# A graph network on one core: indirect transfers ordered by landings in place of clears

## What is computed

```
h = maximum(layernorm(x), 0)
# block 1 (layer 0 below): an equivariant message for each edge, summed at its destination
R = relu(edge_weight[:, None] @ w1 + b1) @ w2 + b2      # 384 radial weights for each edge
Y = spherical_harmonics(edge_attr_3)
msg = tensor product of R, Y and h[src]                 # 32 values
x = x + zeros.at[dst].add(msg)
# block 2 (layers 1 to 3 below): three graph convolutions, 32 -> 128 -> 128 -> 32
h = maximum(layernorm(x), 0)
h = relu(segment_sum((h @ W)[src] * norm[:, None], dst) + b)   # three times
x = x + h
```

## Time and profile before

| | |
|---|---|
| median of 3 runs | 5780.96 us (5775.5 to 5783.35) |
| span of the profiled execution | 5779.7 us |
| its own time beside the span | the trace gives the span alone, first to last instruction; it is 1.3 us below the median |
| busy share of the span | POOL 85%, PE 74%, DVE 62%, PE weight loads 54%, ACT 47% |
| indirect transfers on POOL, L782 | 3616, 1006 ns each |
| clears on POOL, L762 | 3616, 341 ns each |
| DMA queue of the indirect transfers | 109.02 MB in 115712 packets, 10.3% of the 16 engines' time |
| granted TensorE clock, mean over the span | 0.82 of full speed |

### The profile page before, as it was taken

One profiled execution on the slowest core, in us unless ns is written; L12 is line 12 of the kernel. 1 busy time (PEld: TensorE's weight loads), 2 busy tenths in 40 slices (PEclk: granted clock), 3 DMA queues, 4 the chain that ended last, 5 costly groups with the idle time before them and its releaser, 6 DMA issues.

```text
span 5779.7 us, 179150 instructions
## 1 busy us (share of the span) xinstructions
PE 4258.6 (74%) x62463; PEld 3147.7 (54%) x62464; DVE 3608.0 (62%) x8469; ACT 2702.7 (47%) x6550; POOL 4889.1 (85%) x7276
## 2 busy tenths in 40 slices
PE   5777777777777777755555555889898889766666
PEld 3444444444444444444444444778787778554554
DVE  8777777777777777776666666333333334555555
ACT  4444444444444444466666666344444444433333
POOL 7888888888888888768888888688888889588886
PEclk9999999999999999955555555899989999767767
DMA  3111111111111111333332332332333333444444
GB/s 87 33 33 33 33 33 31 33 33 33 33 33 32 32 33 33 36 71 77 77 77 77 77 77 71 114 90 85 91 91 85 91 91 100 119 119 126 122 127 107
DMA packets 494970, 400.88 MB, mean 69 GB/s; under 512 B 269575, under 2 KB 454828, under 8 KB 493537
## 3 DMA queue, kind: packets, MB, share of 16 engines
q10 hardware_dynamic: 146996, 207.67, 10.6%
q0 software_dynamic: 115712, 109.02, 10.3%
q1 hardware_dynamic: 231536, 74.48, 5.9%
HBM read 375.52 MB, written 15.29 MB: 68 GB/s over the span
## 4 chain that ended last, share of the span: by engine, by line
POOL 50%; issue 40%; PE 5%; POOLq 2%; DVE 2%; DMA 1%; ACT 0%; DVEq 0%; SPq 0%
POOL rows L782 29%; POOL pause L762 21%; POOLq L761 2%; PE radial L2067 2%; PE psX L2082 1%; PE psT L2082 1%; PE sums L2153 1%; PE radial L2209 0%; DMA table<-arena 0%; PE radial L2222 0%; DMA rows<-table,idx 0%; DMA xn<-in_x 0%; POOLq L760 0%; PE radial L2008 0%; DVE rows L1827 0%
## 5 line engine op out<-in xcount | busy, mean ns | idle before, releaser
L782 POOL DMA_INDIRECT rows<-table,idx x3616 | 3636.6, 1006 | 803.0 <-POOL pause L762 483.7
L762 POOL MEMSET pause<- 128x256 f32 x3616 | 1234.8, 341 | 2.5
L1942 PEld LDWEIGHTS sums<-scratch,onehot 128*64 128x64 f32 x9408 | 789.7, 144 | 465.0 <-DVE scratch L1377 228.6
L2067 PE MATMUL radial<-arena,shared 128*32 128x96 bf16 (+1 forms) x31200 | 926.4, 266 | 154.2 <-DVE shared L1613 75.1
L1942 PE MATMUL sums<-scratch,onehot 128*64 128x264 f32 (+1 forms) x9408 | 984.1, 356 | 32.6 <-DVE scratch L1377 26.2
L2067 PEld LDWEIGHTS radial<-arena,shared 128*32 128x32 bf16 (+1 forms) x31200 | 664.8, 116 | 294.4 <-issue 72.0
L2153 PE MATMUL sums<-onehot,rows 128*128 128x80 f32 (+1 forms) x2844 | 371.0, 298 | 576.7 <-DMA rows<-table,idx 571.8
L1007 ACT CAST scratch<-radial 128x480 bf16<-128x480 f32 x860 | 476.9, 555 | 665.7 <-PE radial L2067 657.6
L1360 DVE TENSOR_TENSOR scratch<-radial,shared 128x768 f32<-128x768 f32 x784 | 743.4, 948 | 0.0
L1927 PE MATMUL radial<-shared 64*128 64x384 f32 x3136 | 730.5, 546 | 0.0
L880 ACT COPY shared<-rows 128x192 f32<-128x192 f32 x196 | 89.4, 456 | 1264.1 <-DMA rows<-table,idx 1262.9
(11 more groups left out here) (237 smaller groups left out, 5969.3 us busy)
## 6 DMA issues: line engine op xcount, KB each, us to landing
scratch<-places_d ACTq DMA_DIRECT2D x242, 800.0 KB
rows<-table,idx POOLq DMA_INDIRECT x3616
shared<-in_edge_weight SPq DMA_DIRECT2D x390, 128.0 KB, 2.9
idx<-in_src SPq DMA_DIRECT2D x451, 4.0 KB
table<-arena SPq DMA_DIRECT2D x24, 256.0 KB, 2.8
table<-arena SPq DMA_DIRECT2D x2, 1176.0 KB, 10.6
accT<-in_edge_attr SPq DMA_DIRECT2D x2, 1152.0 KB
table<-arena SPq DMA_DIRECT2D x24, 96.0 KB, 2.0
```

Of the source, the lines that this page charges most:

```text
L762: nc.gpsimd.memset(pause[:, :], 0.0).then_inc(made, 1)
L782: (pool.indirect_dma_start(rows_3[:, r, j, :] if n in (1, 3) else rows[:, r, j, 0:WIDTH[n]], None, tables[n], bass.IndirectOffsetOnAxis(ap ...
L1942: last = nc.tensor.matmul(there, onehot[:, u % 2, 4 * h + t, 0:SW], taken_from, start=(h + q + part == 0), stop=(h == 1 and q == 1 and par ...
L2067: last = nc.tensor.matmul(d, from_src[n][:, h, i, t, :], table_of(n, s), start=True, stop=True, tile_position=(0, 32 * i))
```

## The change

The clear, its tile and its counter go. In their place POOL waits ahead of each transfer until the last but one has landed (IN_FLIGHT = 2). To know this of each, the transfers count up two semaphores in turn (LANES = 2): the even tiles j one, the odd ones the other, and no longer one for each place in `rows`. The registers `landed` hold the counts in the loop; in the written-out steps they are constants. Those who wait for a whole group (SP ahead of `load_idx`, ACT, PE) now wait for both semaphores, with `wait_gathered`.

```diff
--- before.py
+++ after.py
@@ -59,7 +59,8 @@
 MSGW = TAIL0 + OUTS
 SUMW = 8 * OUTS
 PAD_REL = -1000.0
-PAUSE = 256
+LANES = 2
+IN_FLIGHT = 2
 assert NG % UNROLL == 0 and PTAIL * KS == ETAIL and PTAIL <= P and NG == 2 * NB
 
 
...
-        pause = sb("pause", [P, PAUSE])
...
@@ -347,7 +347,7 @@
         table_out = sems("table_out", 2)
         chunk_out = sems("chunk_out", 4)
         idx_in = [sem(f"idx_in{u}") for u in range(UNROLL)]
-        gathered = [sem(f"gathered{u}") for u in range(UNROLL)]
+        gathered = sems("gathered", LANES)
         ew_in = sems("ew_in")
         hid_ready = sems("hid_ready", 2)
         rows_copied = sems("rows_copied")
@@ -463,9 +463,11 @@
             n = len(sems)
             return sems[event % n], step.times(step.groups * each // n, before * (UNROLL * each // n) + event // n + 1)
 
-        def rows_gathered(step, n, u, plus):
-
-            return step.times(step.groups // UNROLL * 16 * TPG, 16 * TPG * (rounds_before(n) + u // UNROLL + plus))
+        def wait_gathered(eng, n, step, u):
+
+            each = 16 * TPG // LANES
+            for lane in range(LANES):
+                eng.wait_ge(gathered[lane], step.times(step.groups * each, each * (sum(GATHERED[:n]) + u + 1)))
 
         def bucket_count(n, step, v, plus=0):
 
@@ -614,7 +616,7 @@
                 at = step.times(step.groups * GE, u * GE)
                 if n > 0 or not (first and u < UNROLL):
 
-                    sp.wait_ge(gathered[r], rows_gathered(step, n, u, 0))
+                    wait_gathered(sp, n, step, u - UNROLL)
                 if n == 0 and (step.it * UNROLL + u == NG - 1 if step.peeled else False):
                     d = idx[0:PTAIL, r, 0:KS]
                     s = src[(NG - 1) * GE:E].rearrange("(p k) -> p k", k=KS)
@@ -748,18 +750,18 @@
 
 
             turn = [pool.alloc_register(f"turn_pool{u}") for u in range(UNROLL)]
-            pauses = pool.alloc_register("pauses")
-
-            def pause_between(step, n, u, j):
-
+            landed = [pool.alloc_register(f"landed{lane}") for lane in range(LANES)]
+
+            def wait_landed(step, n, u, j):
+
+                lane = (j - IN_FLIGHT) % LANES
                 if step.peeled:
-                    before = TPG * (sum(GATHERED[:n]) + step.it * step.groups + u) + j
-                    if before:
-                        pool.wait_ge(made, 9 + before)
+                    before = TPG * (sum(GATHERED[:n]) + step.it * step.groups + u) + j - IN_FLIGHT
+                    if before >= 0:
+                        pool.wait_ge(gathered[lane], 16 * (before // LANES + 1))
                 else:
-                    pool.wait_ge(made, pool.snap(pauses))
-                    pool.reg_add(pauses, pauses, 1)
-                nc.gpsimd.memset(pause[:, :], 0.0).then_inc(made, 1)
+                    pool.wait_ge(gathered[lane], pool.snap(landed[lane]))
+                    pool.reg_add(landed[lane], landed[lane], 16)
 
             def gathers(n):
                 def body(step, first, last):
@@ -779,10 +781,10 @@
                             pool.reg_add(turn[r], turn[r], 1)
                         for j in range(TPG):
                             col = j % 2 * KS + j // 2
+                            wait_landed(step, n, u, j)
                             (pool.indirect_dma_start(rows_3[:, r, j, :] if n in (1, 3) else rows[:, r, j, 0:WIDTH[n]], None, tables[n],
                                                      bass.IndirectOffsetOnAxis(ap=idx[:, r, col:col + 1], axis=0))
-                                 .then_inc(gathered[r], 16))
-                            pause_between(step, n, u, j)
+                                 .then_inc(gathered[j % LANES], 16))
                     if n == 0 and first:
                         pool.wait_ge(centred, 2)
                         nc.gpsimd.memset(xn[:, NB - 1, :], 0.0).then_inc(pads, 1)
@@ -804,7 +806,9 @@
                         pool.wait_ge(chunk_out[c % 4], chunks_stored(n, c))
                 for u in range(UNROLL):
                     pool.reg_mov(turn[u], 2 * (LOOP[n][0] // UNROLL - 1) if n else 0)
-                pool.reg_mov(pauses, 9 + TPG * (sum(GATHERED[:n]) + LOOP[n][0]))
+                for lane in range(LANES):
+                    pool.reg_mov(landed[lane], 16 * ((TPG * (sum(GATHERED[:n]) + LOOP[n][0]) + lane) // LANES
+                                                     - (1 if lane >= LANES - IN_FLIGHT else 0) + 1))
                 sweep(pool, body, n)
 
             for n in range(NLAYER):
@@ -873,7 +877,7 @@
                     nc.scalar.activation(hid[:, u % 2, :, :], ew_row[:, u % 2, :].rearrange("c (p k) -> c k p", k=KS),
                                          ACT.Relu, bias=b1c[:, :], scale=w1c[:, :]).then_inc(hid_ready[u % 2], 1)
 
-                    act.wait_ge(gathered[u], rows_gathered(step, 0, u, 1))
+                    wait_gathered(act, 0, step, u)
                     if not (first and u < 2):
                         act.wait_ge(*when(prods_done, step, 4 * (u - 2) + 3, each=4))
                     vec = rows[:, u, :, MUL:F].rearrange("p t (v i) -> p t i v", i=3)
@@ -2142,7 +2146,7 @@
                     counts = [P if j % 2 == 0 else min(P, 2 * used - P) for j in range(TPG)]
                     for j in range(TPG):
                         far_rows[j] = (rows if n == 2 else rows_3)[0:counts[j], r, j, 0:w] if counts[j] else None
-                    pe.wait_ge(gathered[r], rows_gathered(step, n, u, 1))
+                    wait_gathered(pe, n, step, u)
                     far_windows(n, far)
 
                     pe.wait_ge(*when(onehot_ready, step, u, before=rounds_before(n)))
```

## The result

The changed kernel takes 6777.2 us (median of 4 runs, 6759.7 to 6785.3), the kernel before 5778.2 us in the runs beside it: a ratio of 1.173, 95% interval 1.171 to 1.175. The forecast was 6508 us, 12.6% slower; it is 17.3%. The span of the profiled execution is 6783.5 us.

The account below looks back on a forecast made before the run. POOL's issue of the gathers was taken as the bound; with two transfers sharing each L + w, 2540 us for layer 0, 3707 for layers 1 to 3 and 260 outside gave 6508 us, range 6080 to 6830.

Parts of the forecast that it names:

- What bounds the kernel before: POOL, which issues the gathers: transfer, clear and idle time sum to 1.569 us, 3616 times, 5674 us of 5779.7.
- w: On POOL, the time from a transfer's landing until the next transfer can start: 0.80 us, bounds 0.16 and 0.8.
- The first rival: POOL's sequencer prepares a transfer before its wait ends: w 0.16 us, 5350 us in all, 7% faster; chance 0.10.
- the point of no change: The w at which the forecast times before and after the change are equal: 0.40 us.
- L: Time from a transfer's start on POOL to its landing: 2.44 us in layer 0, mean 2.65 in layers 1 to 3.
- The price of a late landing: Layers 1 to 3: late landings cost more than their half, so mean lateness of 0.17 us was charged in full.
- the loop's turns: POOL's idle time of up to 2.35 us at loop turns should hide behind the landing wait; gain left out.
- The sum: Layer 0: 1568 steps of 1.62 us, 2540 us; layers 1 to 3: 2048 of 1.81 us, 3707 us.
- What lies around the layers: The 260 us of the span ahead of, between and behind the layers' stretches of transfers, assumed untouched by the change.
- the clear delays the landing: Rival: the 0.33 us clear behind each transfer is part of L; without it 5910 us; chance 0.07.
- TensorE's clock: Rival: PE is granted the lower clock in layer 0 and sets the time, above 6830 us; chance 0.04.
- late landings vanish: Rival: L is 2.44 us in all layers, giving 6118 us, inside the forecast's range; no separate chance given.

## Why the prediction was right, and where it was too low

**What bounds the kernel before.** Right. A quarter of the clear's columns gave 672 us, from the sum of POOL's pieces alone.

**w.** Right in size and in cause, for the loops: 0.80 was taken from the earlier trace rows, 0.75 is measured. The clear put behind the landing wait cost almost nothing, so the time is the sequencer's. The Trainium skill's figure for a sequencer's dispatch, about 50 ns ("DMA: Bandwidth & Descriptors", section "Anatomy of one DMA — SWDGE (gpsimd) path"), is not what the runs show for an indirect transfer: from the step ahead of it (L764) to the step behind it (L763) the sequencer takes 0.51 us. The step that failed is a smaller one: I took one w for all transfers. The rows of a layer's first transfer behind L807, 0.7 us, didn't show that a wait within the transfer's own instruction ends after the preparation and not ahead of it. In the written-out steps, 576 of the transfers (L764 stands in the trace 3040 times), w is 0.26 us. The first rival (the preparation stays hidden) was thus nearly true of one form of the wait. Even with that form throughout it doesn't carry: with two in flight the kernel is still 7.0% slower than before, although 0.26 is under the 0.40 at which I had put the point of no change. With w at 0.26 my sum gives 4801 + 470 + 260 = 5531 us, and 6179 were measured. What the sum lacks is in the two terms below: the mean L of layers 1 to 3 is 2.91 to 3.13 us in that kernel, and the mean w is some 0.5 us.

**L.** Mis-sized in all layers, by the choice of the transfer. Both values were read from a group's eighth transfer alone, since the consumer waits for that one. For this one they were right: in layer 1 the eighth transfer takes 2.65 us on the mean in the changed kernel, the very value that was taken, and what was subtracted as PE's own start (0.48) shows as 0.49 us in the median from the landing to the matmul in the kernel before. But others of a group land later: the second and third in layer 0 (3.09 and 2.65, beside the edge weights), the third to fifth in layer 1 (2.98 to 3.34), the third to sixth in layer 3 (3.31 to 3.81). So the means are 2.52 for the 2.44 taken in layer 0, and 2.88, 2.95 and 3.07 for the 2.65 taken in layers 1 to 3. This is the largest error of the sum. What makes landings late in layers 1 to 3 was not tested. The Trainium skill's 2.0 us of fixed cost (same page and section) is below the 2.38 to 2.56 us of the medians here.

**The price of a late landing.** Late landings cost more than their half, as I said, since behind a late one all wait in order, and an early landing can't make up for it, because POOL needs 1.25 us anyway (this is argued from the order of the waits, no run shows it alone). But I charged them in full, and that was too much. With the medians of L and w a step in layers 1 to 3 would be 1.61, 1.66 and 1.62 us, the lateness (mean less median) is 0.42, 0.39 and 0.59 us, and the steps are 1.87, 1.89 and 1.95: 0.55 to 0.63 of the lateness came, stalls and turns included. With light weight loads layer 0 fell by 0.57 us a group, of 0.71 us of lateness (0.57 and 0.14) that went: more than half and less than all.

**The stalls and the loop's turns.** I left the turns out as hidden behind the landing wait. The trace has two things here. The larger one I had not seen at all, although the kernel before has it too:

```profile
234.51 0.94 POOL L785 DMA_INDIRECT rows<-table,idx  x1 [0.91 <-DMA rows<-table,idx]
235.80 0.94 POOL L785 DMA_INDIRECT rows<-table,idx  x1 [0.35 <-issue]
240.35 0.95 POOL L785 DMA_INDIRECT rows<-table,idx  x1 [3.61 <-issue]
```

```profile
L764 POOLq ALU_OP  x1: 32/32/32, 236.9 to 236.9; - x1
...
L763 POOLq MOVE  x1: 29/29/29, 240.1 to 240.1; - x1
```

The sequencer takes 3.24 us for this one transfer in place of 0.51. It recurs every 112 transfers, through all layers, 32 times. In the loops it costs 2.7 us each, and some 77 us in all. In the kernel before it comes every 96 transfers and costs 1.5 us; with three or four in flight it comes every 110. It is no turn of a loop: those come every 32 transfers in layer 0, and the kernel with POOL's loops written out has the stall at the same transfers, there 1.9 us:

```profile
388.79 0.96 POOL L785 DMA_INDIRECT rows<-table,idx  x1 [0.90 <-DMA rows<-table,idx]
391.97 0.95 POOL L785 DMA_INDIRECT rows<-table,idx  x1 [2.21 <-issue]
```

What causes it is open. The true turns cost nothing that shows in layers 0 and 3. In layers 1 and 2, one of whose turns is the place of the earlier trace rows, nine of ten cost 1.65 to 5.2 us more than the landing wait, 26 us together; they didn't hide.

**The sum.** Layer 0: 2540 forecast, 2643 measured. By the terms: w at 0.75 for 0.80 is -37 us, L +60, the stalls +35, a wait of 10 us behind the clear of accT at the 33rd transfer (it stands in the kernel before too), and the remaining 35 are late landings over their half, by subtraction. Layers 1 to 3: 3707 forecast, 3883 measured. L is +313, w -46, and the full charge for lateness in place of its half -174. That makes 3800, and of the 83 left the stalls are 42 and the turns 26. So the forecast came as near as it did because two errors in part cancelled: L too low by 313 us and its lateness charged too high by 174. That was luck. With L and w as measured, my own form of the sum would have given 4261 us for these layers, 378 too many. The range held because its upper end was taken with L = 3.13, nothing subtracted, which is near layer 3's true mean. What lies around the layers came out as assumed (257.5 for 260).

**The other rivals.** That the clear delays the landing has fallen: put back behind the transfer, it changed L by 0.01 us. TensorE's clock fell to 0.88 in layer 0, and PE was busy 72% of it, as worked out; it bound nothing. That late landings vanish didn't happen.

## What to carry to other kernels

A wait that replaces a fixed delay costs (L + w) / n for each step, so read both from the trace before you choose n: the landing from the semaphore's records, for every place in the group and not only for the one that a consumer waits for, w from the place where the engine's sequencer meets such an instruction only after a wait. Here two in flight were too few by one, and three or four would have turned a loss of 17% into gains of 6% and 12%. What an engine's sequencer does behind a wait is on the path, even if it is hidden in the kernel as it stands; and ask which instruction holds the wait.

## What the runs showed that I had not expected

- The form of a wait is worth half a microsecond: 0.26 us from landing to start where the wait is in the transfer's instruction, 0.75 us where it is in a register step ahead of it. It makes most of the 598 us that the written-out kernel gained at two in flight.
- Indirect transfers of POOL start no closer than some 1.25 us, with a duration of 0.94 us shown, and a clear of 0.11 us between them is free.
- A written-out program was not slower to fetch than a loop: 5000.6 us against 5063.5 us at four in flight.
- In layer 0 L hardly depends on the number in flight: 2.48, 2.52 and 2.47 us with one, two and four. In layers 1 to 3 it does: 2.63 to 2.69 us with one, 2.88 to 3.07 with two, 2.95 to 3.22 with four.
- POOL's sequencer stalls once in 112 transfers (3.24 us in place of 0.51), in loops and in written-out code alike.
